# Decoder layer pair: self-attention queries and keys kept packed, turned for four sequences at once, spread to the row groups by DMA

## The reference, cut to what matters

```python
# self-attention: 16 heads of 8 channels, causal
q = (x @ Wq.T).reshape(N, L, H, D).transpose(0, 2, 1, 3)    # k, v alike
q = _layernorm(q, gq, bq)                                   # over the 8 channels of a head
k = _layernorm(k, gk, bk)
scores = jnp.einsum('nhld,nhmd->nhlm', q, k)
scores = jnp.where(causal, scores, -1e30)
attn = jax.nn.softmax(scores, axis=-1)
out = jnp.einsum('nhlm,nhmd->nhld', attn, v)
return out.reshape(N, L, EMB) @ Wo.T + bo
# cross-attention on the context: 16 heads of 8, a window
scores = jnp.einsum('bhqd,bhkd->bhqk', qh, kh) / np.sqrt(8)
scores = jnp.where(dist > 64, -jnp.inf, scores)
y = jnp.einsum('bhqk,bhkd->bhqd', softmax(scores), vh)
return y @ W_proj.T + b_proj
# feed-forward: activations and weights rounded to 4-bit floats in blocks of 32, then one matmul
```

## Time and profile before

| | us |
| --- | --- |
| runs | 1454.46, 1456.49, 1458.66 (median 1456.49) |
| profiled execution, its own time | 1459.37 |
| its span in the trace | 1457.6 |
| phase 1, to about | 780 |
| phase 2 | 780 to 939.5 |
| phase 3 | 939.5 to 1457.6, the last slot starting at 1420.6 |

### The profile page before, as it was taken

The page is one execution under the profiler, slowest core; times in us unless marked ns, Lnnn a source line. Parts: engine busy times, 40 slices in busy tenths (PEclk is TensorE's granted clock), DMA queues, the critical chain, the costliest instruction groups (busy, mean ns, idle before and its releaser), DMA issues.

```text
span 1457.6 us, 42538 instructions
## 1 busy us (share of the span) xinstructions
PE 1294.8 (89%) x15257; PEld 942.1 (65%) x15257; DVE 1081.9 (74%) x2573; ACT 1049.3 (72%) x2841; POOL 633.9 (43%) x844
## 2 busy tenths in 40 slices
PE   4358999999999999999984999889889989999995
PEld 1125676666666666767674999856656666676664
DVE  6998889999899988876665344466668778686665
ACT  2128999999999999999981566647666766766653
POOL 0012424353444434310215554448675776655663
PEclk9999999999999999999995999979999999999997
DMA  6942242413214241020112332220101010000000
GB/s 145 242 121 57 52 102 53 113 49 95 66 48 100 52 108 49 16 94 2 52 35 66 101 96 75 96 84 22 32 10 42 11 41 11 26 25 4 25 11 16
DMA packets 83579, 89.00 MB, mean 61 GB/s; under 512 B 15792, under 2 KB 72752, under 8 KB 78768
## 3 DMA queue, kind: packets, MB, share of 16 engines
q1 hardware_dynamic: 77424, 77.10, 20.3%
q0 software_dynamic: 4096, 8.40, 2.0%
q10 hardware_dynamic: 1856, 0.79, 0.2%
HBM read 64.76 MB, written 17.83 MB: 57 GB/s over the span
## 4 chain that ended last, share of the span: by engine, by line
PE 60%; DVE 13%; ACT 10%; issue 8%; POOL 5%; DMA 2%; ACTq 0%; another core or an unknown queue 0%; DVEq 0%; SPq 0%; POOLq 0%
PE P L796 7%; PE P L958 7%; PE P L2114 5%; PE P L1579 4%; PE P L1612 4%; PE P L814 3%; PE P L940 3%; ACT pr L1019 3%; PE P L917 3%; PE P L928 3%; PE P L912 3%; PE P L2176 2%; PE P L2132 2%; PE P L835 2%; PE P L2069 2%
## 5 line engine op out<-in xcount | busy, mean ns | idle before, releaser
L2433 DVE TENSOR_REDUCE mx<-P 128x8 f32<-128x1024 f32 x128 | 156.5, 1223 | 123.8 <-PE P L2114 85.3
L1019 ACT ACTIVATE pr<-P,nm 128x256 f32<-128x256 f32 x512 | 238.6, 499 | 5.9 <-DVE nm L1217 5.7
L2326 ACT ACTIVATE et<-P 128x1024 f32<-128x1024 f32 x128 | 131.0, 1024 | 122.6 <-PE P L2121 110.2
L1217 DVE TENSOR_REDUCE nm<-P 128x4 f32<-128x1024 f32 x128 | 156.1, 1219 | 25.9 <-PE P L796 23.5
L796 PE MATMUL P<-kt_w,qt 64*128 64x256 f32 x1024 | 145.2, 402 | 4.6 <-ACT pr L1019 4.6
L1001 ACT COPY ptS<-P 128x512 f32<-128x512 f32 x256 | 138.1, 598 | 8.7 <-PE P L814 8.4
L992 ACT ACTIVATE pr<-pr,ri 128x256 f32<-128x256 f32 x254 | 119.6, 536 | 24.6 <-DVE pr L1190 24.0
L704 POOL TENSOR_TENSOR kv_qk<-kv_qk,mixing 128x512 f32<-128x512 f32 x48 | 61.0, 1271 | 151.9 <-DVE pr L1190 151.9
L1675 ACT ACTIVATE hT<-P,mixing 128x128 f32<-128x128 f32 x284 | 81.0, 368 | 61.1 <-PE P L1579 56.8
L698 POOL TENSOR_TENSOR kv_qk<-kv_qk,r_w 128x512 f32<-128x512 f32 x48 | 61.0, 1270 | 145.6 <-DVE pr L1190 100.0
L1019 ACT ACTIVATION_READ_ACCUMULATOR pr<-P,nm 128x1 f32 x512 | 118.2, 231 | 0.0
(11 more groups left out here) (351 smaller groups left out, 3652.4 us busy)
## 6 DMA issues: line engine op xcount, KB each, us to landing
kv_qk<-scr_v SPq DMA_DIRECT2D x16, 1024.0 KB, 8.0
r_w<-scr_r SPq DMA_DIRECT2D x16, 1024.0 KB, 10.8
xt<-scr_xs SPq DMA_DIRECT2D x71, 64.0 KB, 1.8
scr_ys<-yt SPq DMA_DIRECT2D x71, 64.0 KB
x<-in_x SPq DMA_DIRECT2D x8, 256.0 KB, 10.2
scr_v<-mixing SPq DMA_DIRECT2D x8, 256.0 KB, 2.5
scr_r<-mixing SPq DMA_DIRECT2D x8, 256.0 KB, 2.0
xb<-in_x SPq DMA_DIRECT2D x8, 256.0 KB, 3.3
```

The lines of the kernel that those rows point to most:

```text
L1019: e = nc.scalar.activation(pr[:, s % 3, h * KEYS:(h + 1) * KEYS], scores(s)[:, h // 2, (h % 2) * KEYS:(h % 2 + 1) * KEYS], ACT.Exp, bias=n ...
L1217: nc.vector.tensor_reduce(nm[:, s % 3, 0:4].rearrange("p (a h) -> p a h", a=2), scores(s).rearrange("p a (h k) -> p a h k", k=KEYS), AX.X, ...
L2326: nc.scalar.activation(et[:, u % 4, :, :, :], scoresT, ACT.Exp).then_inc(S["h_exp"], 1)
L2433: nc.vector.tensor_reduce(mx[:, n % 2, 8 * r:8 * r + 8].rearrange("p (k a) -> p k a", k=2), scores, AX.X, ALU.max, negate=True).then_inc(S ...
```

## The change

Queries and keys of the self-attention are no longer padded. The weight columns of the projection are put in a new order (`wqk`), so that within each of four quarters the channels of the heads interleave. The norm works in place on `qkv`, in two steps again, but each for two sequences with both queries and keys ("norm0", "norm1"). One turn "kt" and one turn "qt" of four 128x128 blocks, one per sequence, then serve all four sequences of a group. ScalarE copies each into `packed` (128x512) with weight and bias. SyncE spreads it: four DMAs, each from 32 partitions of `packed` to 8 partitions and four column blocks of `kTd` or `qTd`. The local queries are turned with one transpose per sequence instead of four, copied 128x128 into `packedE` and spread by four DMAs of 16 KB. The scores contract over 8 partitions, the turned scores over 9, instead of 32. Scores wait for the spreads (`in_sd0`, `in_sd1`, `in_se`) instead of ScalarE's copies.

SyncE's program of phase 3 now waits in a slot for the copy whose result it spreads, and its other issues (local keys, stores, loads) stand behind that. The weight and bias vector (`gbs`) is loaded in phase 1 by 16 small transfers instead of 4; the 1 MB copy of `qS` to `xnE` at the start of phase 3 is gone, and so are four small operations on VectorE in phase 2. The tables change with the steps, and MIDDLE keeps one entry of twelve.

```diff
-        "guess": -19, "inv0": -18, "inv1": -16, "kn": -14, "qn": -13,
-        "qp": None, "kt0": -13, "qt0": -12, "kt1": -11, "kt2": -7, "qt2": -6, "qt1": -5, "kt3": -2, "qt3": -1}
+        "guess": -19, "inv0": -18, "inv1": -16, "norm0": -14, "norm1": -13,
+        "qp": None, "kt": -12, "qt": -11}
...
-        "dxt": 1, "bias": 7, "qk0": None, "qk1": None, "qk2": None, "qk3": None, "qp": 2, "square": 2, "v": 3,
-        "reduce": 3, "guess": 3, "inv0": 4, "inv1": 4, "kn": 5, "qn": 6,
-        "kt0": 6, "qt0": 7, "kt1": 7, "qt1": 8, "kt2": 9, "qt2": 10, "kt3": 11, "qt3": 12},
+        "dxt": 1, "bias": 7, "qk0": None, "qk1": None, "qk2": None, "qk3": None, "qp": 2, "square": 2, "v": 7,
+        "reduce": 3, "guess": 3, "inv0": 4, "inv1": 4, "norm0": 5, "norm1": 5,
+        "kt": 5, "qt": 6},
...
-        "guess": 17, "inv0": 18, "inv1": 19, "kn": 20, "qn": 21,
-        "kt0": 21, "qt0": 22, "kt1": 23, "qt1": 24, "kt2": 25, "qt2": 26, "kt3": 27, "qt3": 28},
+        "guess": 17, "inv0": 18, "inv1": 19, "norm0": 20, "norm1": 20,
+        "kt": 21, "qt": 22},
...
-        "inv0": 30, "inv1": 31, "kn": 34, "qn": 35,
-        "kt0": 35, "qt0": 36, "kt1": 37, "qt1": 38, "kt2": 39, "kt3": 40, "qt2": 41, "qt3": 42},
+        "inv0": 30, "inv1": 31, "norm0": 32, "norm1": 33,
+        "kt": 34, "qt": 35},
...
-                **{62 + 2 * b: ("kt", b) for b in range(GS)}, **{63 + 2 * b: ("qt", b) for b in range(GS)}}
+                62: ("kt", 0), 63: ("qt", 0)}
+FRONT_SPREAD = 69
...
-MIDDLE = (("qt0", 1), ("kt3", 1), ("qt3", 1), ("kt1", 2), ("kt2", 2), ("qt0", 3), ("kt1", 3), ("kt3", 3), ("qt2", 3),
-          ("qt3", 3), ("qt2", 2), ("e2", 7))
+MIDDLE = (("qt", 1),)
...
+        def normed(qkv, g, k, y3):
+
+            x = qkv[:, g % 2, 2 * k:2 * k + 2, :].rearrange("p b (j c a) -> p (b j) c a", c=DH, a=4)
+            nc.vector.tensor_tensor(x, x, bcast(y3[:, 16 * k:16 * k + 16, :], 2, DH), ALU.mult).then_inc(S["d_qkn"], 1)
+
+
+        def spread_heads(sp, dst, src, cols, sem):
+
+            for j in range(4):
+                sp.dma_start(dst[32 * j:32 * j + DH, :, cols], src[32 * j:32 * j + 32, cols]).then_inc(S[sem], 16)
...
                 for s in range(FIRST_H, LAST_H):
+                    for k, (name, dst) in enumerate((("kt", kTd), ("qt", qTd))):
+                        g = self_at(s, name)
+                        if g is not None:
+                            if g >= 2:
+                                sp.wait_ge(S["h_st"], SELF_AT[g - 2] + 8)
+                            sp.wait_ge(S["h7_read"], filled(name, g))
+                            spread_heads(sp, dst[g % 2], packed[:, k, :], slice(0, N), f"in_sd{g % 2}")
+                    for b in range(GS):
+                        g = local_at(s, f"e{b}")
+                        if g is not None:
+                            if g:
+                                sp.wait_ge(S["h_st"], LOCAL_AT[g - 1] + 2 * b + 2)
+                            sp.wait_ge(S["h7_read"], filled(f"e{b}", g))
+                            if g or b:
+                                sp.wait_ge(S["in_se"], local_spread(g, b) - 64)
+                            spread_heads(sp, qTe, packedE, slice(b * T, (b + 1) * T), "in_se")
...
-                        cols, part = slice(b * T, (b + 1) * T), slice(64 * r + 32 * k, 64 * r + 32 * k + 32)
+                        cols, part = slice(b * T, (b + 1) * T), slice(64 * r + 32 * k, 64 * r + 32 * k + DH)
...
-                            nc.scalar.activation(kTd[g % 2][:, :, b * T:(b + 1) * T],
-                                                 bank7.rearrange("p (a n) -> p a n", a=4), ACT.Identity,
-                                                 bias=gbs[:, 5:6], scale=gbs[:, 2:3]).then_inc(S["h7_read"], 1)
...
+                            nc.scalar.activation(packed[:, k, :], bank7, ACT.Identity, bias=gbs[:, 3 - 2 * k:4 - 2 * k],
+                                                 scale=gbs[:, 2 - 2 * k:3 - 2 * k]).then_inc(S["h7_read"], 1)
```

More of the change, by code:

```diff
@@ L1111, in setup @@
                 link(dve, nc.vector.tensor_scalar(hm, hm, 1.0 / DH, None, ALU.mult))
-                link(dve, nc.vector.tensor_tensor(w3, w3, bcast(hm, 2, DH), ALU.subtract))
+                for k in range(2):
+                    spread = wqk[:, k * 128:(k + 1) * 128].rearrange("p (j c a) -> p a j c", j=4, c=DH)
+                    nc.vector.tensor_tensor(spread, wD[:, k * 128:(k + 1) * 128].rearrange("p (a j c) -> p a j c", j=4, c=DH),
+                                            bcast(hm[:, k * H:(k + 1) * H].rearrange("p (a j) -> p a j", j=4), 3, DH), ALU.subtract)
                 link(dve, nc.vector.tensor_scalar(dlt[:, :], pol[:, :], 0.5 * LN2, None, ALU.mult))
@@ L1938, in queries, with self_spread, local_spread @@
                 return qTe if local else qTd[g % 2]
-            def queries_turned(name, g):
-                return max(filled(f"{name}{b}", g) for b in range(GS))
+            def self_spread(g):
+                return 16 * 8 * (g // 2 + 1)
+            def local_spread(g, b):
+                return 16 * 4 * (GS * g + b + 1)
             def head_at(r, t, j):
@@ L1951, in copied @@
             def copied(eng):
[L1952 removed]
+                eng.wait_ge(S["in_g"], 16 * 17)
             def adds_until(s):
@@ L2081, in operands @@
                         turn(bank7, xnD).then_inc(S["h7"], 1)
-                    for b in range(GS):
-                        g = self_at(s, f"kt{b}")
-                        if g is not None and ((f"kt{b}", g) in MIDDLE) == middle:
-                            bank7_free(f"kt{b}", g)
-                            pe.wait_ge(S["d_qkn"], 2 * g + 1)
-                            turn(bank7, quads(kS[:, b])).then_inc(S["h7"], 1)
-                        g = self_at(s, f"qt{b}")
-                        if g is not None and ((f"qt{b}", g) in MIDDLE) == middle:
-                            bank7_free(f"qt{b}", g)
+                    for name, at in (("kt", 128), ("qt", 0)):
+                        g = self_at(s, name)
+                        if g is not None and ((name, g) in MIDDLE) == middle:
+                            bank7_free(name, g)
                             pe.wait_ge(S["d_qkn"], 2 * g + 2)
-                            turn(bank7, quads(qS[:, g % 2, b])).then_inc(S["h7"], 1)
+                            turn(bank7, qkv[:, g % 2, :, at:at + 128]).then_inc(S["h7"], 1)
                     for b in range(GS):
@@ L2097, in operands @@
                             pe.wait_ge(S["e_xn"], GS * g + b + 1)
-                            turn(bank7, quads(xnE[:, b])).then_inc(S["h7"], 1)
+                            nc.tensor.transpose(bank7[:, b * T:(b + 1) * T], xnE[:, b, :], ident[:, :]).then_inc(S["h7"], 1)
                 def maxima(n):
@@ L2189, in tensor_program @@
                                 pe.wait_ge(S["h_add"], adds_until(s))
-                            nc.tensor.matmul(qk_bank, xTd[:, b * T:(b + 1) * T], wD[:, 0:256], start=True,
+                            nc.tensor.matmul(qk_bank, xTd[:, b * T:(b + 1) * T], wqk[:, :], start=True,
                                              stop=True).then_inc(S["qk"], 1)
```

183 lines of the change are left out of this document (72 added, 111 removed).

## The result

Before, four runs have a median of 1456.65 us; the changed kernel took 1517.52, 1520.43, 1524.62 and 1542.23 us. The ratio is 1.044, with a 95% interval of 1.0405 to 1.0477. The forecast was 1440 us, 1427 to 1463: wrong in sign, and the time lies 57 us above the range.

The account below looks back on a forecast made before the run. Phase 3's plain slot pairs hang on scores, VectorE's maximum and the next mask matmul; only other slots can gain. Terms −21.1, −3.2, +5.6, +1.5, +0.85, +1.15, −1.6 sum to −16.8 us: 1440 us against the median 1456.49, range 1427 to 1463.

Parts of the forecast that it names:

- What bounds the kernel, and slot 82: Phase 3: plain pairs stay at 6.41 us; slot 82 gives 0.75 us for the copy and 0.44 for the turn.
- Part 1: Phase 3: 264 transposes and many ScalarE copies go; the share on the path saves 21.1 us of 29.
- the pattern occurs three times, −8.6: Phase 3, slots 78 to 85 and two like stretches: 2.85 us saved in each, −8.6 in all.
- Slots 40 to 42: Phase 3: turns placed in mid-slot delay the weighted sum as well; taking them away saves 2.3 us.
- Part 2: Phase 3 transfers: two stalls go (−3.2), seven loads at new places cost +5.6, spreads +1.5 us.
- The −3.2 for stalls that go: Phase 3: two TensorE waits for row maxima beside local loads vanish as those loads move, saving 3.2 us.
- Part 4: Phase 2: first turn starts up to 1.0 us later, six turns fewer give −2.6; sum −1.6 us.
- Part 5: Scores' contraction over 8 and 9 rows: taken 0, bounds ±5% of 285 ns, which plain slots would hide.
- plain pairs other than 6.41 us: Phase 3 sign of a wrong forecast: it would mean 8-row matmuls have a price of their own.
- a clock of phase 3 under 0.95: Sign of a wrong forecast: TensorE's granted clock in the third phase falls below 0.95.
- Rival A: Phase 3: spreads and moved loads stall maxima transfers; 19 stalls of 2 us cost +38, time 1471 us; chance 0.14.
- Rival C: Phase 3: less TensorE work drops the clock to half; ten falls cost 20 to 50 us, time 1475; chance 0.06.

Follow-up runs that it names:

- e6: Changed kernel with 32-row contraction, no spreads, exponential scaled by 0.001, and VectorE's sum of squares over neighbouring columns: 1444.2 us, ratio 0.9926 to the kernel before.
- e5: Changed kernel with 32-row contraction and no spreads, exponential scaled by 0.001, strided sum kept: 1448.8 us, ratio 0.9950 to the kernel before.
- e2: Changed kernel with contraction back at 32 rows, the added query rows zero, spreads kept: 1484.4 us, ratio 1.0216 to the kernel before.
- e3: Changed kernel without any spread, ScalarE copying turned blocks straight into the first column block; 8 and 9 rows kept: 1472.9 us, ratio 1.0137 to the kernel before.
- e1: Kernel before with only the contraction changed, scores over 8 rows and turned scores over 9: 1465.5 us, ratio 1.0085.
- e4: Changed kernel with VectorE's sum of squares over eight neighbouring columns instead of every fourth: 1507.2 us, ratio 1.0370 to the kernel before.
- e10: Changed kernel with 32 rows and the self-attention's spreads but none for local queries, exponential scaled by 0.001: 1480.3 us, ratio 1.0177 to the kernel before.
- e7: Kernel before with both contractions over 16 rows instead of 32: 1464.9 us, ratio 1.0066.

## Why the prediction was wrong, step by step

By ratios along one path, in us of 1455: savings of turns and copies −10.8 (e6), strided sum +3.5 (e5), spreads +38.7 (e2), fewer rows +32.7 (the changed kernel), together +64. The order matters. Without spreads the rows cost 27 us (e3 against e5), alone in the kernel before 12 (e1); with few rows the spreads cost 44 (e3), the strided sum 10 (e4). Only the step from 12 to 27 or 33 is clear of the intervals: the rows cost more in the new layout, with or without spreads. Which part of the layout does it (turns taken away, strided sum, tables) no run separates.

- **What bounds the kernel, and slot 82**: right. Plain pairs are unchanged, slot 82 gives 1.18 for 1.19.
- **Part 1, −21.1**: right in kind, about twice too large. The term that was mis-sized is "the pattern occurs three times, −8.6": in e6 it gave −3.3 once and nothing twice (−0.1 and +0.2). Three stretches of equal length were taken for equal in what ends last in them; in two of them GpSimd's chain stood right behind ScalarE's. In the changed kernel, behind its delays, slots 48 to 52 and 64 to 68 did give −2.1 and −1.9. Slots 40 to 42 gave −2.3 as forecast: 1146.56 − 1136.16 = 10.40 in the changed kernel for 12.70. The copies out of bank 7 were priced at 0.60 us from a plain copy, though the earlier trace rows has one with scale and bias at 777 ns; they took 777 ns.
- **Part 2, +7.1**: the step that failed first. It lists a spread's bounds as 0 to 2 us for seven places and takes 1.5, on the ground that a spread has 4 issues and a load 17. Issues were the wrong measure: in e10 the 32 small spreads, with twice the issues, cost 6 us and the large ones 33. With 32 rows all spreads cost 38.7 us. The −3.2 for stalls that go was read from rows that don't match: the two waits of the earlier trace rows are in slots 5 and 53, the stall of the earlier trace rows is a third one in slot 61, and slot 5's is counted in part 1 as well. The rule of the Trainium skill that stood beside it, in DMA: Bandwidth & Descriptors, section on queues, rings and completion order, that a completion signal lands only after every earlier write of that DMA engine across its queues, pointed the right way. The runs agree with it in that small transfers landed late beside large ones (slot 63: 6.11 us from issue to scores; by the semaphore's records 12 of 64 took over 3 us to land, before 4), but the trace has no row that shows the order of writes.
- **Part 4, −1.6**: the saving was there. From the first tile to the last e6 takes 136.98 us, the kernel before 138.63. But the spreads behind it were costed only in phase 3. They delayed a store and an input of the experts: the same stretch is 144.00 us in the changed kernel and 137.69 in e5, which lacks them, so they cost 6.3 us. What is moved onto a queue has to be asked of every stage.
- **Part 5, 0 ± 5% hidden by plain slots**: the second step that failed. The duration was about right (a fast 8-row pair keeps its 6.41 us), and the clock was not part of the step at all. Fewer rows cost 12 us alone and 33 in company, over the clock. The sign named for it, plain pairs other than 6.41 us, could not have shown it; the sign that did was the last one named, a clock of phase 3 under 0.95.
- **Rival A** said 1471 with 19 stalls of 2 us and was given 0.14. The waits for maxima were eight, not 19, but single ones reached 4.3 us, and spreads also kept their own scores waiting and slowed phase 2: e2, which has all this without the rows' cost, took 1484. **Rival C**, the clock, was given 0.06 on the ground that the plain pair keeps a clock of 1.00 and that the turns taken away do not count for it; it then priced ten falls at 35 us. The clock fell 15 times in phase 3. With 32 rows, e5 and e6 bear out that ground: 264 transposes fewer and a clock of 0.97 and 0.98. With few rows it stays open. It was wrong to see A and C as alternatives: both came, C behind waits of A (slots 95 to 97) and without them (slots 85 to 88, and e3 with its 102 us at half speed). The point that speaks for C, that the earlier trace rows come behind 3.23 us of idle TensorE, stood in the prediction but not in its sum.
- **The range** took in neither, since each cost was bounded as if it were alone.

What stays open: why a matmul with fewer rows makes the clock fall more easily. e1 and e7 show that it does with everything else equal; no run shows by what. The packed layout with few rows, a plain sum and no spreads was not run; it would tell whether the turns that went make the rows dearer. Nor is it known which of the two spreads of a group, or which of their 2 KB pieces, holds up the maxima.

## What to carry to other kernels

A small transfer on the critical path can be held up by bulk transfers in flight beside it, here by 4.27 us in slot 63: before moving data through DMA to spare TensorE, list every small transfer that somebody waits for and ask what flies beside it. Price anything that makes TensorE idle, or its matmuls smaller, with the slots at half clock that can follow; here slots that waited for transfers cost 20 us and others at a lowered clock 39. And run each part of a change alone: the contraction over fewer rows saved nothing by itself and cost 12 us. And check each occurrence of a "pattern" for what ends last in it, since equal lengths don't mean equal causes.

## What the runs showed of the hardware that was not expected

- The same scores with 8 and 9 or with 16 rows of contraction instead of 32, in an otherwise unchanged kernel, lowered the granted clock of phase 3 from 0.98 to 0.95 and cost 0.85% and 0.66%.
- A sum over every fourth column (128x1024 to 128x128, float32) takes 1,998 ns on VectorE, over neighbours 1,207 ns. A 128x512 copy out of a PSUM bank with scale and bias took 777 ns, a plain one 599.
- The same slots 81 to 85, slot 85 with 5.4 us, left the clock at 1.00 with 32 rows and were followed by a clock of 0.50 in slots 87 and 88 with 8 and 9.
- Two spreads of 4 x 64 KB inside SBUF, from 32 to 8 partitions each, were there 11.5 us after the first issue, of which 5.73 us went into issuing. SyncE needs about 0.7 us to issue one such transfer (2.90 us for four), and no less for one of 16 KB (2.81 us for four), where a load of 16 KB takes 0.36.
